# Selective scan in a decoder kernel: the sums over the states in three parts instead of four, the turning back in a pair slot of its own

## The reference, cut to what matters

```python
A = -jnp.exp(A_log)                                   # 256 x 64
def step(h, inputs):
    d_t, B_t, C_t, u_t = inputs
    dA = jnp.exp(d_t[:, :, None] * A)
    h = h * dA + (d_t * u_t)[:, :, None] * B_t[:, None, :]
    y_t = jnp.einsum('bdn,bn->bd', h, C_t)            # the sum over the 64 states
    return (h, y_t)
y = jnp.transpose(ys, (1, 0, 2)) + u * D
```

## Time and profile before

| | |
|---|---|
| time, three runs | 1402.15, 1405.04, 1410.43 us, median 1405.04 |
| the profiled execution's own time | 1392.17 us |
| its span, first to last instruction | 1390.2 us |
| mean granted TensorE clock | 0.862 of full speed |
| scan, first scanned tile to the end of the last | 80.9 to 406.4 us of the span |
| tiles scanned | 128, in 16 units of 8 |
| DVE, one scan of a tile | 2.26 to 2.29 us |
| POOL, one product of a tile | 2.34 to 2.45 us |
| ACT, one exponential of a tile | about 1.0 us |

### The profile page before, as it was taken

The page is one execution under the profiler, slowest core; times in us unless marked ns, Lnnn a source line. Parts: engine busy times, 40 slices in busy tenths (PEclk is TensorE's granted clock), DMA queues, the critical chain, the costliest instruction groups (busy, mean ns, idle before and its releaser), DMA issues. The chain is left out here.

```text
span 1390.2 us, 29831 instructions
## 1 busy us (share of the span) xinstructions
PE 1040.0 (75%) x12054; PEld 732.3 (53%) x12065; DVE 850.6 (61%) x1500; ACT 525.5 (38%) x1322; POOL 569.6 (41%) x382
## 2 busy tenths in 40 slices
PE   4437777777777989998455796798386989856795
PEld 2126666666764554555245354655285455533595
DVE  7668889889865675466522586567323667745133
ACT  2433444444421553353122173166143757412021
POOL 4079999999946503110345310110533111002232
PEclk9657888778897799999688799799698999978998
DMA  2098778878755000000273000000473000002583
GB/s 105 0 235 215 205 213 212 212 204 216 209 197 178 2 1 0 1 2 1 76 207 116 17 1 1 1 1 2 148 229 122 1 1 2 1 0 75 206 301 102
DMA packets 74231, 139.75 MB, mean 101 GB/s; under 512 B 8128, under 2 KB 28368, under 8 KB 73744
## 3 DMA queue, kind: packets, MB, share of 16 engines
q1 hardware_dynamic: 70128, 129.67, 32.3%
q0 software_dynamic: 3968, 8.18, 1.6%
HBM read 128.06 MB, written 14.82 MB: 103 GB/s over the span
## 5 line engine op out<-in xcount | busy, mean ns | idle before, releaser
L658 ACT ACTIVATE shifted_a<-scores,nmax_a 128x128 f32<-128x128 f32 x768 | 208.6, 387 | 83.2 <-DVE nmax_a L624 83.2
L1204 ACT ACTIVATE decay<-decay 128x1016 f32<-128x1016 f32 x128 | 125.3, 1008 | 193.2 <-PE decay L1128 193.2
L624 DVE TENSOR_REDUCE nmax_a<-scores 128x4 f32<-128x512 f32 x192 | 123.7, 686 | 104.7 <-PE scores L563 102.3
L1128 PE MATMUL decay<-delta,A_pairs 32*128 32x127 f32 x2048 | 96.4, 338 | 102.4 <-DVE small_pack L1223 50.4
L361 POOL TENSOR_TENSOR rstd<-ve,neghalf 128x4 f32<-128x4 f32 x30 | 31.5, 1051 | 280.1 <-DVE ve L347 280.1
L1128 PEld LDWEIGHTS decay<-delta,A_pairs 32*128 32x128 f32 x2048 | 81.4, 234 | 120.1 <-DVE small_pack L1223 50.9
L630 DVE COPY PTs_a<-PT 128x512 f32<-128x512 f32 x192 | 123.4, 681 | 3.2 <-PE PT L571 3.1
L1464 POOL DMA_INDIRECT results<-xs_s x76 | 72.8, 958 | 120.3 <-DVE xs_s L1636 113.0
L571 PE MATMUL PT<-mamba_pack,shifted_a 128*128 128x128 f32 x768 | 112.0, 290 | 3.5 <-DVE PTs_a L630 2.7
L571 PEld LDWEIGHTS PT<-mamba_pack,shifted_a 128*128 128x128 f32 x768 | 87.0, 147 | 35.5 <-issue 19.9
L247 PE MATMUL norm_ps<-identb 128*128 128x512 bf16 x180 | 57.1, 431 | 46.4 <-DVE ve L347 45.7
(11 more groups left out here) (395 smaller groups left out, 2222.5 us busy)
## 6 DMA issues: line engine op xcount, KB each, us to landing
pos_bias<-du_rows SPq DMA_DIRECT2D x72, 256.0 KB, 4.9
small_pack<-L3f_w SPq DMA_DIRECT2D x15, 768.0 KB
XN<-du_rows SPq DMA_DIRECT2D x38, 256.0 KB, 4.7
XNT<-du_rows SPq DMA_DIRECT2D x38, 256.0 KB, 4.8
O<-du_rows SPq DMA_DIRECT2D x36, 256.0 KB, 4.9
masked_cos<-du_rows SPq DMA_DIRECT2D x36, 256.0 KB, 4.8
masked_sin<-du_rows SPq DMA_DIRECT2D x36, 256.0 KB, 4.8
small_pack<-L2f_w SPq DMA_DIRECT2D x15, 514.0 KB
```

What stands on the lines that cost most here:

```text
L624: nc.vector.tensor_reduce(nmax[:, u % 4, :], scores[u % 4][:], AX.X, ALU.min).then_inc(m.maxed, 1)
L658: t = nc.scalar.activation(shifted[u % 4][:, j, :], scores[u % 4][:, j, :], ACT.Exp, scale=-1.0, bias=nmax[:, u % 4, j:j + 1])
L1128: t = nc.tensor.matmul(decay[(2 * p + side) % DEEP][:, s, i, 1:S], A_pairs[strip, c, 4 * q + i, :, :].rearrange("p j n -> p (j n)"), delta ...
L1204: nc.scalar.activation(x, x, ACT.Exp).then_inc(decayed, 1)
```

## The change

The 32 turns of a unit are cut into three parts of 10, 11 and 11, in slots 0, 1 and 2. `turn_back` leaves slot 0 and stands in slot 3 behind `multiply`, where part 3 stood, one slot earlier than before. On ACT `copy_sum` and `place_c` come directly behind the exponential of tile 8n + 15, instead of behind 8n + 17 and 16b + 10, and `copy_y` behind 8n + 18 instead of 8n + 20. The loops end one slot and two tiles earlier.

```diff
-    TURNS = [0, 9, 18, 27, 32]
+    TURNS = [0, 10, 21, 32]
...
-                if part == 3:
+                if part == 2:
                     t.then_inc(summed, 1)
...
-            for p in range(TILES // 2 + 6):
+            for p in range(TILES // 2 + 5):
                 if p < TILES // 2:
                     multiply(p)
-                if p >= 9 and p % 4 == 1:
-                    turn_back((p - 9) // 4)
-                if p >= 5 and (p - 5) // 4 < UNITS:
+                if p >= 8 and p % 4 == 0:
+                    turn_back((p - 8) // 4)
+                if p >= 5 and (p - 5) // 4 < UNITS and p % 4 != 0:
                     gather((p - 5) // 4, (p - 5) % 4)
...
-            for k in range(TILES + 13):
+            for k in range(TILES + 11):
                 if k < TILES:
                     act.wait_ge(multiplied, k + 1)
                     x = decay[k % DEEP][:, :, :, 1:S].rearrange("p s i t -> p (s i) t")
                     nc.scalar.activation(x, x, ACT.Exp).then_inc(decayed, 1)
-                if k % 16 == 10 and 0 < k // 16 < B:
+                if k >= 15 and k % 8 == 7 and (k - 15) // 8 < UNITS:
+                    copy_sum((k - 15) // 8)
+                if k % 16 == 7 and 0 < k // 16 < B:
                     place_c(k // 16)
-                if k >= 17 and k % 8 == 1 and (k - 17) // 8 < UNITS:
-                    copy_sum((k - 17) // 8)
-                if k >= 20 and k % 8 == 4 and (k - 20) // 8 < UNITS:
-                    copy_y((k - 20) // 8)
+                if k >= 18 and k % 8 == 2 and (k - 18) // 8 < UNITS:
+                    copy_y((k - 18) // 8)
```

## The result

The changed kernel took **1381.0 us** in the median of six runs (1371.4 to 1394.0), the kernel before 1403.6 us (1397.2 to 1410.4) in six. The ratio is **0.9846, 95% interval 0.9805 to 0.9887**: 21.6 us faster (the two medians by themselves differ by 22.6). The ratio is that of the fast runs alone, and the longest run of the changed kernel, 1394.0 us, is not one of them.

The account below looks back on a forecast made before the run. The bound was taken to be the multiply, exponential and scan loop, 4.59 us a slot undisturbed, with 25.9 us lost above it. Terms -4.3 - 6.4 - 6.5 + 2.5 = -14.7 us take 1405.0 to 1390 us; range 1383 to 1402.

Parts of the forecast that it names:

- step 5: Unexplained pauses inside parts of the sums on PE, less hidden by 0.8 us of idle: +2.5 us, between 0 and +7.5.
- Step 1: At a unit's first tile, DVE's wait for part 3 of the sums goes: -4.3 us.
- Step 2: Slot 0, relieved of the turning back and with `place_c` a slot earlier, no longer delays the next multiply: -6.4 us.
- Steps 3 and 4: Shorter idle in slots 1 and 2 ends nearly all their slow multiplies, -6.5 us; slot 0's slow multiply stays, 0.
- Steps 6 and 7: ACT's copies and `place_c` delay no exponential, 0; SP's load of `small` and the last gather cost nothing, 0.
- the POOL bound: POOL's busy time of 2.34 us a tile, 18.7 us a unit, limits the gain to 21 us.
- Rival A: Every multiply of slot 0 takes 2.09 us (+4.8), the rest as forecast: gain 9.9 us, 1395 us; chance 0.15.
- Rival B: Feed by POOL and transfers becomes the bound: 3 us gain, 1402 us, or 8.5 us gain; chance 0.15.
- Rival C: PE's clock stays low over most slots, three of four multiplies slow: +12.7 us, 1418 us; chance 0.08.

Follow-up runs that it names:

- u2_place_late: Changed kernel with C placed where it was before, behind the exponential of tile 16b + 10: ratio 0.9957, scan stretch 275.9 us.
- e2_turns: Kernel before with only the sums cut into 10, 11 and 11 turns, turning back left in slot 0, ACT's order as before: ratio 0.9977, stretch 284.1 us.
- e1_place: Kernel before with only C placed earlier, directly behind the copy of the sums (exponential of tile 16b + 9): ratio 1.0038, stretch 281.2 us.
- u1_turn_slot0: Changed kernel with the turning back in slot 0 again, the three-part cut and early placing of C kept: ratio 0.9975, stretch 282.0 us.
- e4_early: Changed kernel with four parts of 5, 9, 9 and 9 turns, the first in slot 3 behind the turning back: ratio 0.9896, stretch 274.5 us.
- f3_early_filled: e4_early with turns that add zeros (1, 2, 2 and 2) put into its parts: ratio 0.9885, stretch 264.0 us.
- f2: Changed kernel with the turning back done four times and one turn of zeros more in part 0: ratio 0.9855, stretch 271.8 us.

## Why the prediction was right or wrong

Direction, place and main mechanism were right. Two things failed: step 5 added 2.5 us for pauses, which the runs put at about nothing, and the low end of the range allowed 1 us for the spread of the runs, where the measurement is uncertain by almost 6 us to either side. Point by point, with the means of the scans:

- **Step 1, the wait at a unit's first tile (-4.3 us): right.** No row of DVE waiting for the sums is left in the changed kernel.
- **Step 2, slot 0 overfull (-6.4 us): right in size.** The slots behind slot 0 have 4.58 or 4.59 us in both kinds of unit, slow multiplies apart. What it rests on was only half seen: the placing of C and the turning back cover one another (u2_place_late), and neither the cut nor the placing is worth anything alone (e2_turns, e1_place).
- **Steps 3 and 4, the clock (-6.5 and 0): right in sum.** The excess of slow multiplies fell from a mean of 16.8 us to 10.3, by 6.5. It is not quite where the forecast put it: of slots 2 and 3 one or two are left in each profile, up to four fell on slot 1, and slot 0 kept 5.4 to 8.2 us instead of 8.1 (11 to 12 in the other two profiles of before).
- **Step 5, the pauses (+2.5 us): this is the term that failed.** Counted as the forecast counted them, by the idle time in the rows, the changed kernel had pauses of 0.5 to 1.7 us in all, not 7.5. Before itself had 7.5, 1.3 and 2.2 us: the forecast took the execution with by far the most as the rule, and charged for idle time that hides less of them. Without the term the sum is -17.2 us, and the seven scans give -17.0. That the two agree so closely is partly luck, since single scans of the changed kernel differ by 6 us.
- **Steps 6 and 7 (0): nothing speaks against them.** `place_c` behind the copy of the sums delayed no exponential, and the load behind the scan delayed nothing.
- **The range: its low end failed.** It stood at the POOL bound of a 21 us gain, 1384 us, with 1 us for the spread of the runs. The bound is one of the scan and held there (14 x 18.7 = 262 us; no stretch was shorter than 262.9). But the whole time moves by more than the scan: the interval of the first comparison alone is 5.7 us to either side. Of the 9 us by which the forecast missed, 2.5 are step 5 and 1.4 the median of before, which was 1403.6 us in six runs and not 1405.0. The other 5 or so are within the spread. Where they arose is not shown: in the profiled pair the scan gave 20.1 us, 3 more than the mean, and the other stages lost 10.6.
- **Rival A** (the clock takes everything of slot 0) did not come, though it describes u1_turn_slot0. **Rival B** (the feed) fell: POOL was busy for 97% of the stretch with no wait of DVE for it. (Before has two such waits, 1.6 us in all, which the prediction's list of waits leaves out.) The rule of the Trainium skill ("Perfetto Trace Analysis", "Identifying the Most-Contended Engine"), to improve the engine with the highest occupancy first, points to POOL here. POOL was busy for 90% of the stretch in before, and yet the order on PE, busy for 74% of it, gave 17 us. **Rival C** (slow over most slots) is e4_early's case in part: 24 of 56.

What the pauses are can be read from the traces. Number all records of TensorE in order, weight loads and sequencer records among them: all 87 pauses of the 17 profiles come at the same place of a block of 256 records (remainder 194 after division by 256, or 193 in 15 cases). The DMA queue that the profile calls "q8 instruction" moves one packet of 16384 bytes for each such block (103 for the 26473 records of f3_early_filled, 96 for the 24670 of before), and each pause ends 1.3 to 1.7 us after the end of such a packet (the one in the earlier trace rows, at 297.94, 1.4 us after). The queue on the profile page of f3_early_filled, with packets, MB and share:

```profile
q8 instruction: 103, 1.69, 0.5%
```

So a pause is, by all that the traces show, PE waiting for its next block of instructions. A block lasted 6.1 to 6.3 us on average in the changed kernel, 6.6 in before, and 5.4 and 5.3 in f2 and f3, which have the most instructions and 14 pauses each. Not settled: why before had seven in one execution and four in each of the other two.

## What to carry to other kernels

Where an engine works in short slots beside a loop that waits for it, removing its waits may only move idle time ahead of the next critical operation, and the clock takes the gain back. It matters which work stands behind a long idle stretch, and what is cheap at the lower clock. Undo each part of such a change by itself before crediting it: here the three parts are worth 17 us together, and two of them nothing alone (the third was not run alone). And take a term of a forecast from more than one execution: the pauses of the one profile of before were the exception.

## What the runs showed of the hardware

- At the same real work, 56 added TensorE instructions a unit raised the granted clock of the stretch from 0.85 to 0.98 (e4_early, f3_early_filled; over the whole kernel 0.854 to 0.861 in eight runs, 0.872 to 0.886 in six). The stretch was 10.5 us shorter in the two profiles; the whole time did not differ beyond the intervals.
- The multiply (32 rows of the array, 127 columns) takes 2.09 us at the 1.2 GHz level and 1.17 at 2.4. The sums (128 rows, 64 columns, four column groups in turn) take about 30 ns an instruction at either: 80 in 2.43 us at the lower level, 72 in 2.19 us at the higher.
- The clock fell behind even idle stretches of 1.3 us that recurred every 4.6 us (24 slow multiplies of 56 in e4_early), and seldom behind 0.8 us (6 slow of the 112 in slots 2 and 3 of the changed kernel, four profiles).
- TensorE paused inside streams of matmuls, with 0.4 to 2.8 us from one start to the next and from 0 to 14 times in 56 slots. All 87 pauses stand at one place of a block of 256 instruction records, 1.3 to 1.7 us after a packet of 16384 bytes on the instruction queue had ended.
